# Attention block on one Trainium2 core: the work of four slots put into two unlike steps, and the output stores issued by ScalarE

## The reference, cut to what matters

```
x: (16, 32, 32, 512) float32           # 16 batches of 1024 tokens, 512 channels
h = group_norm(x, 32 groups, eps 1e-6) * scale + bias
qkv = h @ qkv_w + qkv_b                # 512 x 1536
q, k, v = split(qkv, 3);  q, k *= 1/sqrt(sqrt(64))
q, k, v -> (16 * 8, 1024, 64)          # plain reshapes of (16, 1024, 512)
w = softmax(q @ k.T);  a = w @ v
out = x + (a -> (16, 1024, 512)) @ proj_w + proj_b
```

## Time and profile before

| | |
|---|---|
| median of 3 runs | 3506.1 us (3504.74 to 3506.66) |
| the profiled execution | 3506.26 us |
| its span, first to last instruction | 3504.5 us |
| TensorE matmul busy | 3454.0 us, 99% |
| VectorE busy | 2782.3 us, 79% |
| ScalarE busy | 2062.2 us, 59% |
| GpSimd busy | 1626.9 us, 46% |
| granted TensorE clock, mean | 0.998 |
| q1, the queue of SP: share of 16 DMA engines | 76.5% |

### The profile page before, as it was taken

One profiled execution on the slowest core, in us unless ns is written; L12 is line 12 of the kernel. 1 busy time (PEld: TensorE's weight loads), 2 busy tenths in 40 slices (PEclk: granted clock), 3 DMA queues, 4 the chain that ended last, 5 costly groups with the idle time before them and its releaser, 6 DMA issues.

```text
span 3504.5 us, 67790 instructions
## 1 busy us (share of the span) xinstructions
PE 3454.0 (99%) x24640; PEld 2515.0 (72%) x24640; DVE 2782.3 (79%) x3473; ACT 2062.2 (59%) x3985; POOL 1626.9 (46%) x2762
## 2 busy tenths in 40 slices
PE   6999999999999999999999999999999999999998
PEld 4777777777777777777777777777777777777775
DVE  4878878888788787887888788887878878888776
ACT  5566566565565665655656656556556566565563
POOL 4454444454444444444544444445454444444452
PEclk9999999999999999999999999999999999999999
DMA  4777778777787878777777787877777778777777
GB/s 126 191 182 190 187 186 191 181 190 184 187 192 182 191 181 191 186 187 189 183 190 188 182 193 179 195 183 186 190 183 190 184 187 191 181 191 185 178 180 171
DMA packets 255707, 646.87 MB, mean 185 GB/s; under 512 B 73872, under 2 KB 73872, under 8 KB 255376
## 3 DMA queue, kind: packets, MB, share of 16 engines
q1 hardware_dynamic: 254224, 638.35, 76.5%
q10 hardware_dynamic: 1152, 4.19, 0.3%
HBM read 71.84 MB, written 33.55 MB: 30 GB/s over the span
## 4 chain that ended last, share of the span: by engine, by line
PE 91%; POOL 3%; ACT 2%; DVE 1%; issue 1%; SPq 1%; DMA 0%; POOLq 0%; ACTq 0%
PE pv_ps L399 26%; PE s_ps L369 22%; PE c_ps L439 7%; PE c_ps L440 6%; PE c_ps L441 6%; PE c_ps L422 4%; PE c_ps L450 4%; PE c_ps L452 3%; PE c_ps L424 3%; PE c_ps L423 3%; PE c_ps L451 3%; PE pv_ps L380 2%; PE s_ps L472 2%; ACT staged L519 1%; ACT probs L501 1%
## 5 line engine op out<-in xcount | busy, mean ns | idle before, releaser
L632 DVE TENSOR_REDUCE neg_max<-s_ps 128x1 f32<-128x1024 f32 x1024 | 1204.6, 1218 | 642.0 <-PE s_ps L369 642.0
L501 ACT ACTIVATE probs<-s_ps,neg_max 128x1024 f32<-128x1024 f32 x1024 | 1143.6, 1117 | 938.8 <-DVE neg_max L632 935.4
L615 DVE STREAM_TRANSPOSE turned<-probs 128x1024 f32<-128x1024 f32 x1024 | 1231.2, 1226 | 40.5 <-ACT probs L501 6.0
L399 PE MATMUL pv_ps<-probs_t,v 128*64 128x256 f32 x8192 | 999.9, 386 | 9.6 <-DMA probs_t<-turned 9.6
L399 PEld LDWEIGHTS pv_ps<-probs_t,v 128*64 128x64 f32 x8192 | 544.6, 137 | 347.0 <-issue 117.6
L439 PE MATMUL c_ps<-h_hi,w_hi 128*128 128x256 f32 x2048 | 606.7, 296 | 10.3 <-POOL h_lo L742 6.4
L440 PE MATMUL c_ps<-h_lo,w_hi 128*128 128x256 f32 x2048 | 579.3, 283 | 0.0
L441 PE MATMUL c_ps<-h_hi,w_lo 128*128 128x256 f32 x2048 | 579.1, 283 | 0.0
L519 ACT ACTIVATE staged<-c_ps,qk_bias 64x256 f32<-64x256 f32 x1024 | 479.7, 468 | 18.2 <-PE c_ps L441 4.7
L439 PEld LDWEIGHTS c_ps<-h_hi,w_hi 128*128 128x128 f32 x2048 | 391.1, 191 | 102.6 <-issue 96.6
L755 POOL CAST qh_e<-staged 128x256 fp32r<-128x256 f32 x256 | 102.4, 400 | 648.8 <-ACT staged L519 648.8
(11 more groups left out here) (71 smaller groups left out, 5171.3 us busy)
## 6 DMA issues: line engine op xcount, KB each, us to landing
probs_t<-turned SPq DMA_DIRECT2D x4096, 128.0 KB, 2.3
x_res<-in_x SPq DMA_DIRECT2D x128, 256.0 KB, 2.9
result<-x_res SPq DMA_DIRECT2D x128, 256.0 KB, 2.0
x_next<-in_x SPq DMA_DIRECT2D x120, 256.0 KB, 2.9
probs_t<-in_L_conv_qkv_w ACTq DMA_DIRECT2D x4, 768.0 KB, 8.7
turned<-in_x SPq DMA_DIRECT2D x4, 512.0 KB, 13.1
probs_t<-in_L_conv_proj_w ACTq DMA_DIRECT2D x4, 256.0 KB, 13.8
v_bias<-in_L_conv_qkv_b SPq DMA_DIRECT2D x1, 256.0 KB, 16.9
```

What stands on the lines that cost most here:

```text
L399: last = nc.tensor.matmul(pv_ps[side][CH * par:CH * (par + 1), 0, :], v_sb[:, ring_of(i, parity), CH * chunk:CH * (chunk + 1)], p_t[:, par ...
L501: nc.scalar.activation(probs[k % 2][:, :], s_ps[k % 2][:, :], ACT.Exp, bias=neg_max[:, k % 4:k % 4 + 1], accum_out=row_sum[:, (k // HALF) ...
L615: nc.vector.transpose(dst, probs[k % 2][:, :].rearrange("p (k b j) -> p k b j", k=CHUNKS, b=QUADS)).then_inc(probs_turned, 1)
L632: nc.vector.tensor_reduce(neg_max[:, k % 4:k % 4 + 1], s_ps[k % 2][:, :], AX.X, ALU.max, negate=True).then_inc(max_ready, 1)
```

## The change

- TensorE goes in steps of two slots. A step at a multiple of four does two score tiles, then all large units of four slots, then the spreading; the other step does two score tiles, then all 32 matmuls of `attend`, then a group average if one is due.
- `large_unit` is replaced by a table `LARGE`: slot 0 of 16 makes both v tiles (now for the pair that is attended, one pair later than before); slots 4 and 12 a q/k unit, a projection unit and a q/k unit; slot 8 four q/k units. The q/k tiles come in the order q, q, k, k, q, q, k, k. Slot numbers of the statistics move to multiples of four, `small` stands before the third large unit.
- The lags change: spreading of half n in step 4n+8 (it was 9), attending in 4n+10 (it was 9 and 11).
- ScalarE stages the q/k units between and behind its two exponentials, and issues the output store, in steps 6 and 14 of 16; SP issued it before. SP's load of the residual tile, which waits for the store, stays in slots 7 and 15.
- GpSimd does the work of four slots at once, with widening at the end, for half n in its turn at slot 4n.

```
-MOVE_LAG = 4
-WIDEN_LAG = 7
-ATTEND_LAG = 9
+LARGE = {0: [("v", 0), ("v", 1)], 4: [("qk", 0), ("proj", 0), ("qk", 1)],
+         8: [("qk", 2), ("qk", 3), ("qk", 4), ("qk", 5)], 12: [("qk", 6), ("proj", 1), ("qk", 7)]}
+QK_TILES = [0, 1, 4, 5, 2, 3, 6, 7]
+SMALL_BEFORE = 2
+MOVE_LAG = 4
+SPREAD_LAG = 8
+ATTEND_LAG = 10
 EVAC_LAG = 12
...
 # TensorE
+            def step(b, k):
                 s = SPB * b + k
+                if within(s, N_SLOTS):
                     scores(b, k)
                     scores(b, k + 1)
-                large(b, k)
-                small(b, k)
-                if k % HALF == ATTEND_LAG % HALF and within(s - ATTEND_LAG, N_SLOTS):
-                    spread_inverse(b, k)
-                    attend(b, k, 0)
-                if k % HALF == (ATTEND_LAG + 2) % HALF and within(s - ATTEND_LAG - 2, N_SLOTS):
-                    attend(b, k - 2, 1)
+                if k % HALF == 0:
+                    for i, (kind, n) in enumerate(LARGE[k % 16]):
+                        if i == SMALL_BEFORE:
+                            small(b, k)
+                        make[kind](b, k, i, n)
+                    if within(s - SPREAD_LAG, N_SLOTS):
+                        spread_inverse(b, k)
+                else:
+                    if within(s - ATTEND_LAG, N_SLOTS):
+                        attend(b, k)
+                    small(b, k)
...
 # ScalarE
+            def store(b, n):
+                h = BLOCKS * b + n
+                if within(h, N_BLOCKS):
+                    act.wait_ge(out_ready, h + 1)
+                    act.dma_start(out_t[h // BLOCKS, h % BLOCKS], x_res[:, :]).then_inc(stored, 16)
...
                 if within(s, N_SLOTS):
                     softmax_exp(b, k)
+                if k % 16 == 8:
+                    stage_qk(b, k, 0)
+                if within(s, N_SLOTS):
                     softmax_exp(b, k + 1)
...
+                if k % 16 == 4 or k % 16 == 12:
+                    stage_qk(b, k, 0)
+                if small_unit(k)[0] == "stats" and within(b + 1, BATCHES):
+                    copy_x(b, k)
+                if k % 16 == 4 or k % 16 == 12:
+                    stage_qk(b, k, 2)
+                if k % 16 == 8:
+                    stage_qk(b, k, 1)
+                    stage_qk(b, k, 2)
+                    stage_qk(b, k, 3)
+                if k % 16 == 6:
+                    store(b, 2 * (k // 16) - 2)
+                if k % 16 == 14:
+                    store(b, 2 * (k // 16) - 1)
...
 # GpSimd
             def widen_inverse(b, k):
-                n = (k - WIDEN_LAG) // HALF
+                n = k // HALF
...
-            def slot(b, k):
+            def four_slots(b, k):
                 m, pair = k % 16, k // 16
+                if m == 4 or m == 12:
+                    split_qk(b, k, LARGE[m][0][1])
+                if m == 8:
+                    split_qk(b, k, LARGE[m][0][1])
+                    split_qk(b, k, LARGE[m][1][1])
+                split_attn(b, (k - EVAC_LAG) // HALF)
+                if m == 0:
+                    add_bias(b, 2 * pair - 2)
+                if m == 0 and within(made_pair(b, k), N_PAIRS):
+                    split_h(b, k)
...
+                if m == 8:
+                    add_bias(b, 2 * pair - 1)
+                if m == 4 or m == 12:
+                    split_qk(b, k, LARGE[m][2][1])
+                if m == 8:
+                    split_qk(b, k, LARGE[m][2][1])
+                    split_qk(b, k, LARGE[m][3][1])
+                widen_inverse(b, k)
+                if k == GROUP_MEAN_SLOT and within(b + 1, BATCHES):
                     affine(b)
...
+            batches(lambda b, k: four_slots(b, k) if k % HALF == 0 else None)
```

More of the change, by code:

```diff
@@ L239, in moved_count, with bank, emptied @@
             return 64 * (half // 2 + 1)
-        units = [k for k in range(SPB) if large_unit(k)[2] == 0]
+        units = [(k, i) for k in range(0, SPB, HALF) for i in range(len(LARGE[k % 16]))]
         small_ps = s_ps[0][:, 0:C]
[L246 to L250, removed]
+        def bank(k, i):
+            return c_ps[units.index((k, i)) % 2]
+        def emptied(b, k, i):
+            kind, n = LARGE[k % 16][i]
             if kind == "proj":
-                h = proj_block(b, k)
+                h = proj_block(b, k, n)
                 return within(h, N_BLOCKS), out_ready, h + 1
@@ L314, in load_residual @@
                     sp.dma_start(x_res[:, :], x_t[b + n // BLOCKS, n % BLOCKS]).then_inc(x_loaded, 16)
[L316 to L320, removed]
             def move_half(b, k):
@@ L382, in spread_inverse, with attend @@
                 last.then_inc(inv_full, 1)
-            def attend(b, k, part):
+            def attend(b, k):
                 n = (k - ATTEND_LAG) // HALF
@@ L387, in attend @@
                 i, parity = (n // 2) % 2, (n // 4) % 2
[L388 to L395, removed]
+                for quad in range(QUADS):
+                    pe.wait_ge(moved[n % 2][quad], 64 * (BLOCKS * b + n // 2 + 1))
+                if n % 4 == 0:
+                    pe.wait_ge(v_ready, 2 * (PPB * b + n // 4) + 1)
+                if n % 4 == 2:
+                    pe.wait_ge(v_ready, 2 * (PPB * b + n // 4) + 2)
+                for kt in range(8):
                     chunk = 2 * (kt % 4) + kt // 4
@@ L403, in attend @@
                             start=(kt == 0), stop=(kt == 7))
[L404 to L426, removed]
-                    return
[L428 to L442, removed]
-                    return
-                if not within(v_pair(b, k), N_PAIRS):
@@ new lines, in attend, with project @@
+                last.then_inc(pv_done, 1)
+            def project(b, k, i, n):
+                h, c = proj_block(b, k, n), bank(k, i)
+                if not within(h, N_BLOCKS):
+                    return
+                if h == 0:
+                    pe.wait_ge(w_ready, 2 * KT)
+                pe.wait_ge(attn_ready, 2 * h + 2)
+                await_bank(pe, b, k, i)
+                for j in range(KT):
+                    a_hi = attn_hi[:, j // 2, (j % 2) * P:(j % 2 + 1) * P]
+                    a_lo = attn_lo[:, j // 2, (j % 2) * P:(j % 2 + 1) * P]
+                    nc.tensor.matmul(c[:, :], a_hi, pw_hi[:, j, :], start=(j == 0), stop=False)
+                    nc.tensor.matmul(c[:, :], a_hi, pw_lo[:, j, :], start=False, stop=False)
+                    last = nc.tensor.matmul(c[:, :], a_lo, pw_hi[:, j, :], start=False, stop=(j == KT - 1))
+                last.then_inc(proj_full, 1)
@@ new lines, in make_qk @@
+            def make_qk(b, k, i, n):
+                g, c, tile = made_pair(b, k), bank(k, i), QK_TILES[n]
+                if not within(g, N_PAIRS):
+                    return
+                if before_start(b) and n == 0:
+                    pe.wait_ge(w_ready, KT)
+                await_bank(pe, b, k, i)
+                for t in range(KT):
+                    if n == 0 and t % 2 == 0:
+                        pe.wait_ge(h_split, 2 * g + t // 2 + 1)
+                    wh, wl = (w[:, t, tile * P:(tile + 1) * P] for w in (w_hi, w_lo))
+                    nc.tensor.matmul(c[:, 0:2 * P], wh, h_hi[:, t, :], start=(t == 0), stop=False)
+                    nc.tensor.matmul(c[:, 0:2 * P], wh, h_lo[:, t, :], start=False, stop=False)
+                    last = nc.tensor.matmul(c[:, 0:2 * P], wl, h_hi[:, t, :], start=False, stop=(t == KT - 1))
+                last.then_inc(qk_full, 1)
@@ L445, in large, with make_v @@
+            def make_v(b, k, i, n):
+                if not within(attended_pair(b, k), N_PAIRS):
                     return
-                if part == 0:
-                    await_bank(pe, b, k)
-                for t in (2 * part, 2 * part + 1):
+                c = bank(k, i)
+                await_bank(pe, b, k, i)
+                for t in range(KT):
                     hh, hl = (h[:, t, n * P:(n + 1) * P] for h in (h_hi, h_lo))
@@ L452, in large @@
                     last = nc.tensor.matmul(c[:, :], hl, w_hi[:, t, 2 * C:3 * C], start=False, stop=(t == KT - 1))
-                if part == 1:
-                    last.then_inc(v_full, 1)
+                last.then_inc(v_full, 1)
             def small(b, k):
@@ L478, in small @@
                                      start=True, stop=True).then_inc(group_full, 1)
[L480 removed]
+            make = {"v": make_v, "qk": make_qk, "proj": project}
+            def step(b, k):
                 s = SPB * b + k
[L482 removed]
+                if within(s, N_SLOTS):
                     scores(b, k)
                     scores(b, k + 1)
[L485 to L491 removed]
+                if k % HALF == 0:
[9 more added lines that the diff above has]
+                    small(b, k)
             pe.wait_ge(const_made, 2)
[L494 removed]
+            batches(in_steps(step))
         @block.scalar
@@ L504, in softmax_exp, with stage_qk @@
                                      ).then_inc(probs_ready, 1)
-            def stage_qk(b, k, n):
```

(16 more changed lines are left out.)

125 lines of the change are left out of this document (39 added, 86 removed).

## The result

The changed kernel takes 3668.48 us (3661.95 to 3670.1, 4 runs) against 3506.14 us: 4.6% slower, ratio 1.046, 95% interval 1.0442 to 1.0478. The forecast was 3660. The profiled execution took 3661.95 us, with a span of 3660.2, 155.7 more than before.

The account below looks back on a forecast made before the run. TensorE, busy 99% of the span, was taken to bound the kernel. 3506 - 84 (shape) + 13 (small waits) + 126 (GpSimd late) + 72 (batch ends) + 25 (clock) = 3658, rounded 3660 us; 8 in 10 range 3570 to 3735.

Parts of the forecast that it names:

- Shape changes: TensorE: two changes of the array's tile shape go in four slots, 0.33 us, 84 us in all (51 to 102).
- small waits: TensorE in slots 4: third unit waits for the first unit's bank; with the group average 0.8 a batch, 13 us (0 to 25).
- GpSimd late, ScalarE behind it: Widening waits for late spreading; ScalarE's stagings delay exponentials; TensorE waits 1.7 + 0.4 us, 63 times: 126 us (76 to 176).
- Batch ends: Late statistics, group average, variance and affine cost 4.8 us at each of 15 batch ends: 72 us (0 to 110).
- The affine's part: GpSimd's affine stands behind slot 44's widening, delaying ScalarE's normalising and the bank for slot 52: 2.1 us a batch.
- the group average and the variance: Group average waits for slot 44's exponential, slot 48's scores for the variance: 2.7 us a batch beyond the 2.0.
- Stores: Output stores issued by ScalarE, with SP's residual load waiting behind: some moves start late, but nothing counted.
- The clock: TensorE's granted clock falls after a third of 63 waits, 1.2 us lost each: 25 us (0 to 76).
- the reading that each wait lets the clock fall: TensorE's clock falls at every wait, 76 us; part of the third rival, with VectorE's lateness: 3761 us, chance 0.07.
- The first rival: GpSimd isn't late enough to matter, as ScalarE's stages or exponentials have more slack: 3450 us, chance 0.10.

Follow-up runs that it names:

- The three engines' own edits: Changed kernel with one edit each: spreading ahead of large units (TensorE) 3441.48 us; widening one half later (GpSimd) 3462.95; two late stagings behind exponentials (ScalarE) 3509.88.
- the two versions without lateness: Changed kernel with the spreading ahead of the large units, 3441.48 us, and changed kernel with the widening one half later, 3462.95 us.

## Why the prediction was right, step by step

- **Shape changes.** Counted 0.33 us in four slots, bounds 0.20 to 0.40. The run that puts two like them back gives 0.34. The sum holds too: with the lateness gone the kernel takes 63 us less than before, and -84, the 13 us of small waits and 8 us of a wait at the batch ends (below) make -63.
- **GpSimd late, ScalarE behind it.** The shown slot 8 has no small transposes, so the prediction's times are 0.44 less: widening at 7.9 (measured 7.95), third staging at 9.6 (9.60), scores of slot 12 at 14.7 (14.73), waits of 1.7 and 0.4 (1.72 and 0.30). Counted 126 us; at the 1.8 us of the waiting step and the 0.4 by which the step behind it is longer than with the widening later (8.46 for 8.04 us in slots 12 and 28, falls of the clock left out) it is 2.2 us a pair, 139 us. The three engines' own edits each take away the part that stands behind them.
- **Batch ends.** Counted 4.8 us, and too much. The affine's part is 1.8 us for 2.1. For the group average and the variance I had 2.7. The step of slot 44 is 1.6 us longer than with the widening later, 0.4 of it the pair's, and those of slots 46 and 48 are not longer. The wait for the variance in slot 48 is there, 0.5 us, but it isn't GpSimd's lateness: it stands in the list of waits of the run with the spreading first too, and in that of the kernel before it doesn't:
```profile
PE s_ps L344 <- DVE gvar L700: 8.2, 15, 0.6
```
  Together 1.8 + 1.2 + 0.5 = 3.5 us a batch, 53 us for the 72.
- **Not counted.** The place of the spreading behind the large units costs 21 us, as the two versions without lateness show. The prediction has no term for it.
- **Stores.** Counted nothing; nothing that can be told from none was measured.
- **The clock.** Lost clock is the span times what the clock lacks: 3660 x 0.008 - 3504 x 0.002 = 22 us, where I took 25. But a loss of clock is not yet time. One wait in three was too many: 11 of 60 waits were followed by a fall (9 of the 57 shorter ones, 2 of the 3 of 2.0 us). Ten of these are in the steady part. Six cost 1.5 us each, where I took 1.2; the four in a step with the group average cost nothing: 9 us. Some 6 more of clock are lost in the first 280 us of the span, where the mean is 0.97 and was 0.99; so the term is 9 to 15 us. One of the two of 2.0 us (the wait, and the 4 us from there on, clock third from last):
```profile
1559.54 0.50 PE L344 MATMUL s_ps<-kh,qh_e 64*128 64x512 f32 x2 [2.00 <-ACT probs L475]
```
```profile
1559.00:1563.00 4.00, 3.32 (x16) 2.10 (x17) 3.44 (x8) 1.85 (x5) 2.83 (x6) 0.73 0.00 0
```
This one is in a slot 44 and cost nothing. The other of 2.0 us cost 1.5: its step lasts 9.93 us, where that of the same kind from 1504.23 us to 1512.70, without a fall, lasts 8.47:
```profile
1896.94 0.50 PE L344 MATMUL s_ps<-kh,qh_e 64*128 64x512 f32 x2 [2.00 <-ACT probs L475]
...
1906.87 0.51 PE L344 MATMUL s_ps<-kh,qh_e 64*128 64x512 f32 x2
```
So the reading that each wait lets the clock fall, which the Trainium skill's sentence stood for ("TensorE: Matmul & The Clock Gate", Part 1), did not hold at 1.7 us and did, but for one wait, at 2.9, where the clock lost 3781 x 0.031 = 117 us, 88 more than after the change (3660 x 0.008 = 29), of which some 50 are time.

With these sizes the sum is -84 + 13 + 139 + 53 + 21 + 15 = 157 us, where the spans differ by 155.7. The mechanism is the one forecast. That the total came within 9 us is in part luck: what the batch ends and the clock have too much, some 30 us, is made up for by the place of the spreading and by the pairs' 13 us more.

The first rival was the one to fear, and the run with the spreading moved shows what it would have been: 3441 us, against the 3450 that I gave it.

## What to carry to other kernels

When work is regrouped in larger steps, look for each wait at the end of a queue's turn and ask in which turn of the other engine its release now stands: a lag that was written in small slots changes sign when the slots grow. Read such a wait along the queue behind it, for the engine that waits (GpSimd, half idle) is seldom the one that pays. And try the release first: moving two small products by 6 us in TensorE's queue gave back 227 us, more than the 162 that the change had cost.

## What was not expected of the hardware

- From waits of 1.7 to 2.0 us to waits of 2.9, TensorE's granted clock went from a fall behind 11 of 60 to a fall behind 58 of 59, and 1.16 us of lateness cost 114 / 63 = 1.8.
- A fall of the clock cost 1.5 us in a step without another wait (9.95 us for 8.46) and nothing in the step with the group average (9.97 both ways).
- A step with two transposes on the whole array lasted 0.06 us longer with them between large units and scores (7.75 us) than between scores and large units (7.69).
